# Carrying the negative row maxima into the query stacks by VectorE and DRAM instead of TensorE and ScalarE, in a fused attention kernel

## The reference

```
Q, K, V = x Wq.T + bq, ctx Wk.T + bk, ctx Wv.T + bv       16 heads of 32
att     = softmax(Q K.T / sqrt(32))                       per batch and head
x1      = layernorm(att V Wo.T + bo + x) * gamma0 + beta0
phi(z)  = elu(z)
KV      = phi(ctx).T ctx ;  Z = 1 / (phi(x1) . sum(phi(ctx)) + 1e-6)
out     = layernorm(x1 + (phi(x1) KV) Z) * gamma1 + beta1
```

## Time and profile before

| what | us |
|---|---|
| median of three executions | 1755.48 |
| the profiled execution | 1762.24 |
| its span, first to last instruction | 1760.9 |
| TensorE matmuls busy | 1646.2 |
| VectorE busy | 1070.9 |
| ScalarE busy | 880.9 |
| GpSimd busy | 951.3 |

### The profile page before, as it was taken

The page is one execution under the profiler, slowest core; times in us unless marked ns, Lnnn a source line. Parts: engine busy times, 40 slices in busy tenths (PEclk is TensorE's granted clock), DMA queues, the critical chain, the costliest instruction groups (busy, mean ns, idle before and its releaser), DMA issues.

```text
span 1760.9 us, 32310 instructions
## 1 busy us (share of the span) xinstructions
PE 1646.2 (93%) x12176; PEld 1114.6 (63%) x12176; DVE 1070.9 (61%) x2216; ACT 880.9 (50%) x1617; POOL 951.3 (54%) x923
## 2 busy tenths in 40 slices
PE   6999999999999999999999999999999999999754
PEld 4667776676766666567666657657676767665321
DVE  2665557656666666567566756666666666666232
ACT  0355547555554554654554554665545554575321
POOL 0244535455655664455665655555566555566644
PEclk8999999999999999999999999999999999999877
DMA  8524162233315244141523234322322423200001
GB/s 252 159 63 132 55 204 78 73 99 103 108 40 138 79 130 162 55 115 39 144 79 110 74 103 146 110 85 91 112 72 91 122 74 102 97 24 13 25 24 36
DMA packets 149291, 168.05 MB, mean 95 GB/s; under 512 B 12816, under 2 KB 111120, under 8 KB 149136
## 3 DMA queue, kind: packets, MB, share of 16 engines
q1 hardware_dynamic: 149136, 165.99, 31.8%
HBM read 124.00 MB, written 41.94 MB: 94 GB/s over the span
## 4 chain that ended last, share of the span: by engine, by line
PE 81%; DVE 6%; POOL 4%; DMA 4%; issue 3%; ACT 2%; SPq 1%; DVEq 0%; ACTq 0%; POOLq 0%
PE acc L300 13%; PE score L258 13%; PE scoreT L282 12%; PE misc L375 6%; PE misc L329 6%; PE misc L367 6%; PE acc L308 6%; PE misc L339 6%; PE misc L351 5%; PE misc L319 4%; DVE maxes L553 2%; POOL pair_sum L760 1%; PE score L267 1%; DMA res_out<-ctx_nat 1%; DMA ctx_nat<-ctx_in 1%
## 5 line engine op out<-in xcount | busy, mean ns | idle before, releaser
L760 POOL TENSOR_TENSOR pair_sum<-p_ring 128x512 f32<-128x512 f32 x512 | 654.5, 1299 | 636.0 <-PE acc L308 568.5
L553 DVE TENSOR_REDUCE maxes<-score 128x1 f32<-128x512 f32 x1024 | 679.1, 678 | 441.6 <-PE score L258 440.5
L451 ACT ACTIVATE p_ring<-scoreT 128x512 f32<-128x512 f32 x1024 | 595.6, 594 | 616.8 <-PE scoreT L282 603.5
L258 PE MATMUL score<-k_stack,q_stack 96*128 96x512 f32 x1024 | 615.6, 603 | 8.7 <-DVE maxes L553 7.5
L282 PEld LDWEIGHTS scoreT<-q_stack,k_stack 104*128 104x128 f32 x2048 | 378.7, 191 | 187.8 <-ACT p_ring L451 114.4
L282 PE MATMUL scoreT<-q_stack,k_stack 104*128 104x256 f32 x2048 | 428.0, 291 | 16.3 <-ACT p_ring L451 14.8
L258 PEld LDWEIGHTS score<-k_stack,q_stack 96*128 96x128 f32 x1024 | 194.3, 190 | 170.4 <-issue 139.2
L300 PE MATMUL acc<-p_ring,v_sb 128*32 128x256 f32 x4096 | 279.4, 392 | 0.0
L300 PEld LDWEIGHTS acc<-p_ring,v_sb 128*32 128x32 f32 x4096 | 155.5, 112 | 81.6 <-ACT p_ring L451 22.2
L308 PE MATMUL acc<-pair_sum,ones 128*32 128x256 f32 x2048 | 159.3, 383 | 7.7 <-POOL pair_sum L760 7.7
L319 PE MATMUL misc<-xT_sb,wq 128*128 128x256 f32 x512 | 134.3, 386 | 10.1 <-DVE k_low L615 5.8
(11 more groups left out here) (66 smaller groups left out, 1221.8 us busy)
## 6 DMA issues: line engine op xcount, KB each, us to landing
xT_sb<-xT_in SPq DMA_DIRECT2D x64, 512.0 KB, 4.1
k_stack<-k_dram SPq DMA_DIRECT2D x96, 256.0 KB, 4.4
q_stack<-q_dram SPq DMA_DIRECT2D x192, 128.0 KB, 2.5
ctxT_sb<-ctxT_in SPq DMA_DIRECT2D x8, 1024.0 KB, 7.3
k_dram<-k_high SPq DMA_DIRECT2D x32, 256.0 KB, 2.0
k_dram<-k_low SPq DMA_DIRECT2D x32, 256.0 KB, 2.6
q_dram<-q_high SPq DMA_DIRECT2D x64, 128.0 KB, 1.7
q_dram<-q_low SPq DMA_DIRECT2D x64, 128.0 KB, 1.9
```

The lines of the kernel that those rows point to most:

```text
L258: pe.matmul(score[use % 3][:], q_stack[0:SPLIT, unit % NQ, j, t * P:(t + 1) * P], k_stack[0:SPLIT, unit // NC % 2 * QUAD + j, h * HALF:(h ...
L451: act.activation(p_ring[:, n % NP, h * HALF:(h + 1) * HALF], scoreT[k % 2][:], ACT.Exp, scale=SCALE).then_inc(A["exped"], 1)
L553: dve.reduce_max(maxes[:, unit % 2, t, j, h:h + 1], score[bank_use[k] % 3][:], AX.X).then_inc(V["maxed"], 1)
L760: pool.tensor_tensor(pair_sum[:, pair % 2, cols], p_ring[:, (n - 1) % NP, cols], p_ring[:, n % NP, cols], ALU.add).then_inc(L["paired"], 1)
```

## The change

The negative maxima no longer pass through TensorE, PSUM and ScalarE. VectorE writes the split maxima into the first 16 of 32 columns of one buffer `neg_max`, and in step 3 turns that buffer in blocks of 32 by 32 into `max_turned`. SyncE writes the four blocks to DRAM with four DMAs (`put_max`, at step 4) and reads them back with one DMA that repeats the rows for the four heads in `q_stack` (`stack_max`, at step 6). Pass 2 waits for that DMA (`max_in`). The lead of pass 2 over pass 1 grows from 22 to 26 steps and the visits go with it, to steps 7 and 15 (`VISIT_AT = 39`); so do the steps of `normalise`, now 0 to 3, and the planner's dates are moved by 2 or 4 steps. `stack_queries` stands 4 steps later (step 10). The three score banks serve pass 1 alone.

```diff
-    LEAD = 22
-    PLACE = 19
-    VISIT_AT = 35
+    LEAD = 26
+    VISIT_AT = LEAD + 13
@@ storage
-        neg_max = sb("neg_max", [P, 2, TPC, 2 * QUAD], F32R)
+        neg_max = sb("neg_max", [P, DK], F32R)
+        max_turned = sb("max_turned", [P, 2, DK])
+        max_dram = nc.dram_tensor("max_dram", [2, 2 * QUAD * TPC, P], F32).ap()
@@ planner
-                return UT * NC * (i // 2) - 36 + 8 * (i % 2) if i > 1 else FIRST
+                return UT * NC * (i // 2) - 32 + 8 * (i % 2) if i > 1 else FIRST
-            spaced = UT * UB * b + 242 + TILE_TICKS * t
-            return max(UT * unit + 50, spaced if b < B - 1 else 0)
+            spaced = UT * UB * b + 246 + TILE_TICKS * t
+            return max(UT * unit + LEAD + 28, spaced if b < B - 1 else 0)
@@ TensorE, pass1
-                if use >= 3:
-                    pe.wait_ge(*bank_freed[use - 3])
+                if k >= 3:
+                    pe.wait_ge(V["maxed"], k - 2)
@@ TensorE
-            def place_max(unit):
-                use = bank_use["max", unit]
-                pe.wait_ge(V["max_split"], unit + 1)
-                pe.wait_ge(*bank_freed[use - 3])
-                for t in range(TPC):
-                    mm = pe.matmul(score[use % 3][SPLIT:ROWS, t * P:(t + 1) * P],
-                                   neg_max[:, unit % 2, t, :].bitcast(F32), ident[:],
-                                   start=True, stop=True, tile_position=(0, SPLIT))
-                mm.then_inc(T["max_turned"], 1)
@@ TensorE, pass2
-                    pe.wait_ge(A["max_placed"], unit + 1)
+                    pe.wait_ge(M[f"max_in{unit % 2}"], landed(unit, 2, 1))
@@ ScalarE
-            def place_max(unit):
-                use = bank_use["max", unit]
-                act.wait_ge(T["max_turned"], unit + 1)
-                if unit >= NQ:
-                    act.wait_ge(T["scoredT"], UT * (unit - NQ + 1))
-                act.activation(q_stack[SPLIT:ROWS, unit % NQ, :, :],
-                               score[use % 3][SPLIT:ROWS, 0:CH].unsqueeze(1).to_broadcast([2 * QUAD, QUAD, CH]),
-                               ACT.Copy).then_inc(A["max_placed"], 1)
@@ VectorE, split_max
+                parts = neg_max[:, 0:TPC * 2 * QUAD].rearrange("p (r t) -> p t r", t=TPC)
+                else:
+                    dve.wait_ge(V["max_split"], unit + 1)
+                    if unit >= 2:
+                        dve.wait_ge(M[f"max_out{u}"], landed(unit - 2, 2, QUAD))
+                    dve.transpose(max_turned[:, u, :], neg_max[:].bitcast(F32)).then_inc(V["max_turned"], 1)
@@ VectorE, main loop
-                if 0 <= unit < UNITS and i < 3:
+                if 0 <= unit < UNITS and i < 4:
                     split_max(unit, i)
@@ SyncE
+            def put_max(unit):
+                sp.wait_ge(V["max_turned"], unit + 1)
+                if unit >= 2:
+                    sp.wait_ge(M[f"max_in{unit % 2}"], landed(unit - 2, 2, 1))
+                for block in range(QUAD):
+                    sp.dma_start(max_dram[unit % 2, :, block * DK:(block + 1) * DK],
+                                 max_turned[block * DK:block * DK + 2 * QUAD * TPC, unit % 2, :]
+                                 ).then_inc(M[f"max_out{unit % 2}"], 16)
+
+            def stack_max(unit):
+                sp.wait_ge(M[f"max_out{unit % 2}"], landed(unit, 2, QUAD))
+                sp.dma_start(q_stack[SPLIT:ROWS, unit % NQ, :, :].bitcast(F32),
+                             max_dram[unit % 2].rearrange("(r t) n -> r (t n)", t=TPC).unsqueeze(1).to_broadcast(
+                                 [2 * QUAD, QUAD, CH])).then_inc(M[f"max_in{unit % 2}"], 16)
@@ SyncE, main loop
+                unit, i = divmod(k - UT - 4, UT)
+                if i == 0 and 0 <= unit < UNITS:
+                    put_max(unit)
+                if i == 2 and 0 <= unit < UNITS:
+                    stack_max(unit)
-                unit, i = divmod(k + 10, UT)
+                unit, i = divmod(k + 6, UT)
                 if i == 0 and NQ <= unit < UNITS:
                     stack_queries(unit)
```

More of the change, by code:

```diff
@@ L139, in landed @@
             return 16 * each * (index // slots + 1)
-        bank_use, bank_freed = {}, []
-        for k in range(HALVES + PLACE):
-            if k < HALVES:
-                bank_use[k] = len(bank_freed)
-                bank_freed.append((V["maxed"], k + 1))
-            if k % UT == PLACE % UT and k >= PLACE:
-                bank_use["max", (k - PLACE) // UT] = len(bank_freed)
-                bank_freed.append((A["max_placed"], (k - PLACE) // UT + 1))
         LENGTH = {"K": 4, "V": 4, "Q": 2, "O": 4, "T": 1, "A": 4, "S": 8, "N": 1, "B": 4}
@@ L173, in earliest @@
             unit = UB * b + UB - NC + t // TPC
-            spaced = UT * UB * b + 242 + TILE_TICKS * t
-            return max(UT * unit + 50, spaced if b < B - 1 else 0)
+            spaced = UT * UB * b + 246 + TILE_TICKS * t
+            return max(UT * unit + LEAD + 28, spaced if b < B - 1 else 0)
         def deadline(kind, i):
-            late = {"K": -18, "V": 34, "Q": -14}.get(kind)
+            late = {"K": -18, "V": 36, "Q": -14}.get(kind)
             if kind in "KV":
@@ L254, in pass1 @@
                             pe.wait_ge(M[f"k_in{half}"], landed(unit // NC, 1, 3))
-                use = bank_use[k]
-                if use >= 3:
-                    pe.wait_ge(*bank_freed[use - 3])
-                pe.matmul(score[use % 3][:], q_stack[0:SPLIT, unit % NQ, j, t * P:(t + 1) * P],
+                if k >= 3:
+                    pe.wait_ge(V["maxed"], k - 2)
+                pe.matmul(score[k % 3][:], q_stack[0:SPLIT, unit % NQ, j, t * P:(t + 1) * P],
                           k_stack[0:SPLIT, unit // NC % 2 * QUAD + j, h * HALF:(h + 1) * HALF],
                           start=True, stop=True).then_inc(T["scored"], 1)
-            def place_max(unit):
-                use = bank_use["max", unit]
-                pe.wait_ge(V["max_split"], unit + 1)
-                pe.wait_ge(*bank_freed[use - 3])
-                for t in range(TPC):
-                    mm = pe.matmul(score[use % 3][SPLIT:ROWS, t * P:(t + 1) * P],
-                                   neg_max[:, unit % 2, t, :].bitcast(F32), ident[:],
-                                   start=True, stop=True, tile_position=(0, SPLIT))
-                mm.then_inc(T["max_turned"], 1)
             def pass2(k):
@@ L424, in tensor_program @@
                 beside(k)
-                unit, i = divmod(k - PLACE, UT)
-                if i == 0 and 0 <= unit < UNITS:
-                    place_max(unit)
                 v, i = divmod(k - VISIT_AT, 2 * VISIT)
@@ L552, in maximum @@
                     dve.wait_ge(V["max_whole"], unit - 1)
-                dve.reduce_max(maxes[:, unit % 2, t, j, h:h + 1], score[bank_use[k] % 3][:],
+                dve.reduce_max(maxes[:, unit % 2, t, j, h:h + 1], score[k % 3][:],
                                AX.X).then_inc(V["maxed"], 1)
@@ L567, in split_max @@
                     dve.wait_ge(V["max_whole"], unit + 1)
-                    if unit >= 2:
-                        dve.wait_ge(T["max_turned"], unit - 1)
-                    dve.tensor_copy(neg_max[:, u, :, 0:QUAD], max_row[:]).then_inc(V["max_high"], 1)
-                else:
-                    dve.wait_ge(V["max_high"], unit + 1)
-                    dve.tensor_tensor(neg_max[:, u, :, QUAD:2 * QUAD], max_row[:],
-                                      neg_max[:, u, :, 0:QUAD].bitcast(F32),
-                                      ALU.subtract).then_inc(V["max_split"], 1)
+                    if unit > 0:
+                        dve.wait_ge(V["max_turned"], unit)
+                    dve.tensor_copy(parts[:, :, 0:QUAD], max_row[:]).then_inc(V["max_high"], 1)
+                elif stage == 2:
+                    dve.wait_ge(V["max_high"], unit + 1)
+                    dve.tensor_tensor(parts[:, :, QUAD:2 * QUAD], max_row[:], parts[:, :, 0:QUAD].bitcast(F32),
+                                      ALU.subtract).then_inc(V["max_split"], 1)
+                else:
+                    dve.wait_ge(V["max_split"], unit + 1)
+                    if unit >= 2:
+                        dve.wait_ge(M[f"max_out{u}"], landed(unit - 2, 2, QUAD))
+                    dve.transpose(max_turned[:, u, :], neg_max[:].bitcast(F32)).then_inc(V["max_turned"], 1)
             def normalise(unit, stage):
@@ L708, in vector_program @@
                     onehot[SPLIT:ROWS, :].unsqueeze(2).to_broadcast([2 * QUAD, QUAD, S])).then_inc(V["hot_rows"], 1)
+            dve.tensor_copy(neg_max[:], onehot[:, 0:1].to_broadcast([P, DK])).then_inc(V["pad_cleared"], 1)
+            dve.wait_ge(V["pad_cleared"], 1)
             dve.wait_ge(M["cols"], 3 * 16)
```

8 lines of the change are left out of this document (4 added, 4 removed).

## The result

The changed kernel is slower: median 1771.77 us (1767.8 to 1772.9, four executions) against 1756.99 (four executions) of the kernel before. The ratio is 1.0077, 95% interval 1.0051 to 1.0103: a small loss, but outside the noise. The forecast was 1732, range 1710 to 1755. Two single executions, one of 2359.85 us of the kernel before and one of 8667.07 us of an experiment, are in no ratio of this document.

The account below looks back on a forecast made before the run. The prediction took TensorE's work at full clock as the bound, with VectorE setting the pace in light units. Its terms, -26.2 - 8 + 3 + 5 + 2 = -24 us, gave 1732 us, range 1710 to 1755.

Parts of the forecast that it names:

- term 2: TensorE's wait for VectorE's split before the placing of the maxima goes; half of 15.8 us credited, 8 us gained.
- term 3: Maxima's way through DRAM to pass 2: in time in full units, sometimes late in light ones; 3 us lost.
- Term 1: The matmuls placing the maxima on TensorE go: 0.41 us per unit, 64 units, 26.2 us gained.
- The dead heat in light units: Rows of maxima and TensorE's first pass 2 both arrive 9.9 us after step 0; 3 us lost.
- term 4: SyncE's queue, once in the first batch: eight context loads issued ahead of the maxima's write; 5 us lost.
- Term 5: Fill and drain: four more steps with only pass 1, four more with only pass 2; 2 us lost.
- The third rival: The trip through DRAM is long: landing 5.3 us in place of 1.7, 1803 us at its end; chance 0.08.
- The clock: Rival: thin TensorE stretches in light units drop the clock, 1750 to 1765 us; chance 0.13, shared with late maxima.

Follow-up runs that it names:

- without the way at lead 22: Kernel before less the placing of maxima on TensorE; maxima split and turned but not carried, lead, visits and normalise unmoved: 1717.64 us, ratio 0.9763.
- without it at lead 26: Changed kernel without the five DMAs per unit that carry the maxima and without pass 2's wait for them: 1751.8 us, ratio 0.9964.

## Why the prediction was wrong

Two steps failed: term 2, the overlap, where the move of `normalise` onto the split was priced at 8 us of gain and cost 34, and term 3, the trip, priced at 3 us and measured at 20. Term by term, the sum of -26.2 - 8 + 3 + 5 + 2 became -26 for the matmuls, -16 for the wait, +34 for the move (the longer fill and drain in it) and +20 for the trip (the collision in it).

**Term 1** (-26.2) was right: 0.40 us per full unit, by the chain.

**Term 2** (-8) failed, as a step and not in size alone. I took half of the wait for the split as won and called the rest unchanged. Without the move the whole of the 15.8 us went (42 us in all, of which 26 are matmuls), and nothing came in its place; the weight loads' number, 32.1 us, my outer bound, was twice too large. With the move as much came back as bank waits, 23.4 against 23.3 us by the matmuls, 58.1 against 57.1 by the weight loads, and the rest of the 34 us on top. I had seen that split and normalise now shared four steps, and summed it for a light unit: visit begun 5.7 us after step 0, measured 212.95 - 206.56 = 6.4. Two things were missing. One is which half of a unit holds the projection, so that many units with side work elsewhere are light in steps 0 to 7; I named the two projections as what absorbs the lag, and did not see that they stand in steps 14 and 15. The other is the duration of the split, for which I took 0.08 us of chain from one quiet unit where the two group rows of before gave 0.27 and 0.29, and where the place behind the visit of step 15, beside GpSimd's additions, makes it 0.58 and 0.50. The edits that undid the one or the other gave 20 to 24 us each.

**Term 3** (+3) was mis-sized: 20 us. The write landed in 1.7 us at the median, as I had it from the earlier trace rows, but up to 6.8, and the price is made by those: in 33 of the 64 units SyncE issued a load of keys, xT, context or weights, each of 256 KB or more, between the last 4 us ahead of the first write and the read. All 13 places where a pass 2 waited for the rows are among them, and none among the other 31. The dead heat in light units, for which the 3 us stood, made none of these waits by itself. The largest single wait, 6.28 us, and the half clock behind it:

```profile
71.33 0.79 PE L263 MATMUL scoreT<-q_stack,k_stack 104*128 104x256 f32 x2 [6.28 <-DMA q_stack<-max_dram]
...
71.92 1.91 PE L310 MATMUL misc<-ctxT_sb,wk 128*128 128x512 f32 x2
```

SyncE had issued it behind a wait for keys and three loads of `k_stack`:

```profile
63.22 0.44 SPq L887 DMA_DIRECT2D k_dram<-k_low  x1
65.56 1.28 SPq L895 DMA_DIRECT2D k_stack<-k_dram  x3
66.88 0.38 SPq L877 DMA_DIRECT2D q_stack<-max_dram  x1
```

I had priced a collision with the context loads only (**term 4**, +5); the wait there was 1.76 us, and the keys, in every group of units, and xT, in every unit, were the real neighbours. A median to landing says nothing of a DMA that is issued behind 768 KB. **Term 5** (+2) was 4.3 for the drain alone: from the last pass 1 to the last pass 2 34.9 us before and 39.2 after. Its windows (busy us by engine, clock), before and after:

```profile
1616.40:1651.30 34.90, 29.96 (x226) 18.11 (x227) 12.79 (x32) 19.48 (x34) 22.87 (x22) 0.90 0.05 16
```

```profile
1622.60:1661.80 39.20, 34.03 (x278) 19.75 (x277) 14.35 (x39) 20.25 (x36) 27.61 (x26) 0.89 0.05 16
```

**Small pieces.** The rule on pieces under 512 bytes (the Trainium skill, "DMA: Bandwidth & Descriptors", "Specifications") did not decide: the 2 KB in pieces of 128 bytes landed in 1.7 us at the median, as the 128 KB of queries did in pieces of 1 KB. The third rival, with a landing of 5.3 us, was not what happened, though the sign was its.

**The clock** played a part that no run isolates. Behind the light unit's wait the visit took 3.44 us for its first 32 instructions against 1.86, at a clock of 0.55:

```profile
212.90:216.40 3.50, 3.50 (x37) 1.70 (x40) 1.01 (x2) 0.60 (x1) 0.00 (x0) 0.55 0.04 11
```

In the changed kernel nine of the ten such stretches at 1.2 GHz between 100 and 1600 us came behind a wait of TensorE of 0.28 to 2.6 us, so some waits cost more than their rows say. The traces bound their share. Added up over the clock's rows, TensorE was busy at 1.2 GHz for 60 us in the kernel before, 61 without the way at lead 22, 75 without it at lead 26, and 87 in the changed kernel. If all that work would have taken half as long at the full clock, the clock is at most 7 of the move's 34 us and 6 of the trip's 20; that is an estimate from these sums.

**A reading.** The earlier trace rows show three slices below 9 tenths at the end (8, 7, 7), where I wrote of the last two. No term uses it.

## What to carry to other kernels

When a stage is moved in a hand-written schedule, list for the stretch it moves into what every engine has there: the side work that used to cover it, and what a neighbour engine does at that moment. A wait that is removed is won only if nothing else reaches the same point as late; the run that removes it and moves nothing tells what it is worth, here 16 us beside the 26 of matmuls where I credited 8, and the run that moves it shows what comes back, here 34. And before two small DMAs are put on a queue, read what is issued just ahead of them: the order of issues was worth 50 us in one of these kernels.

## What the runs showed of the hardware

Two VectorE operations on 128x8 elements, from SBUF to SBUF, took 0.15 us each in the quiet and up to 1.27 (the cast) and 1.29 us (the subtraction) while GpSimd worked on SBUF. Taken one by one in the trace of the changed kernel, the 31 that no instruction of GpSimd overlapped took at most 0.16 us, the 97 others 0.64 and 0.69 at the mean. Moved next to GpSimd's additions their means were 0.58 and 0.50 us, moved away 0.33 and 0.22. The reduction of 128x16 elements beside them stayed at 0.15 to 0.16 us at the mean throughout, and the 128x32 turn at 0.19 in that trace, with GpSimd or without.

Four matmul instructions with 8 stationary columns cost TensorE 0.41 us ahead of 32-column matmuls on other column groups, and 0.73 us ahead of a pass 1 with 128 stationary columns. That they overlap the former and not the latter fits the chain, which gives them 0.21 us there and 0.53 here; it was not tested further.
